# Two semaphores instead of one for the clearing of sixteen row regions

## The reference

```
x = x + 0.5 * moe0(layernorm(x))      # 8 experts, hidden 176, top 2, plus a shared expert of 352
x = x + hgrn(layernorm(x))            # gated linear recurrence, four 256x256 projections
x = x + 0.5 * moe0(layernorm(x))      # the same weights again
x = x + 0.5 * moe1(layernorm(x))      # 16 experts, hidden 128, top 2, plus a shared expert of 128
x = x + attention(layernorm(x))       # 4 heads of 64, sequences of 256
x = x + 0.5 * moe1(layernorm(x))

def moe(X):                           # silu(X W1) * (X W3), then W2, for each chosen expert
    scores = sigmoid(X @ gate); idx = top_k(scores + bias, 2)
    w = scores[idx] / sum(scores[idx])
    return sum_k w[k] * expert[idx[k]](X) + shared(X)
```

## Time and profile before

| what | us |
|---|---|
| runs of the kernel | 882.50, 883.11, 884.25 (median 883.11) |
| profiled execution: span from first to last instruction | 880.5 |
| PE busy in the span | 777.2 (88%) |
| DVE busy | 501.6 (57%) |
| ACT busy | 420.1 (48%) |
| POOL busy | 299.5 (34%) |

### The profile page before, as it was taken

One profiled execution on the slowest core, in us unless ns is written; L12 is line 12 of the kernel. 1 busy time (PEld: TensorE's weight loads), 2 busy tenths in 40 slices (PEclk: granted clock), 3 DMA queues, 4 the chain that ended last, 5 costly groups with the idle time before them and its releaser, 6 DMA issues.

```text
span 880.5 us, 14544 instructions
## 1 busy us (share of the span) xinstructions
PE 777.2 (88%) x3982; PEld 553.5 (63%) x3982; DVE 501.6 (57%) x1737; ACT 420.1 (48%) x1020; POOL 299.5 (34%) x316
## 2 busy tenths in 40 slices
PE   5989999999898996999984699998899886899991
PEld 3446777764465454777752468886677664578881
DVE  4656322368866654322368663227897866663248
ACT  4812334317735711334326436553688777246550
POOL 1570433400000372333314717551011133627560
PEclk9999999999999997999995799999999998899996
DMA  8843333199999523333177235536000011245528
GB/s 297 260 148 104 113 108 96 54 303 366 343 344 341 177 102 119 103 106 104 55 258 299 106 120 178 157 109 222 1 1 2 0 50 42 90 135 185 156 98 290
DMA packets 102364, 135.26 MB, mean 154 GB/s; under 512 B 11366, under 2 KB 90726, under 8 KB 101734
## 3 DMA queue, kind: packets, MB, share of 16 engines
q1 hardware_dynamic: 87894, 95.05, 33.5%
q0 software_dynamic: 14400, 39.34, 12.6%
HBM read 56.23 MB, written 78.12 MB: 153 GB/s over the span
## 4 chain that ended last, share of the span: by engine, by line
PE 64%; DVE 16%; ACT 6%; issue 4%; POOL 4%; DMA 4%; SPq 1%; DVEq 0%; POOLq 0%; ACTq 0%
PE bank L1001 20%; PE bank L1022 12%; PE bank L895 9%; PE bank L981 4%; POOL slot_rows L507 4%; PE bank L1012 3%; PE bank L1067 2%; PE bank L908 2%; DVE X L1295 2%; DVE X L1299 2%; PE bank L835 2%; DVE st L1313 2%; PE bank L1118 2%; DMA Y<-f_result_rows 1%; PE bank L1186 1%
## 5 line engine op out<-in xcount | busy, mean ns | idle before, releaser
L507 POOL DMA_INDIRECT f_result_rows<-arena x172 | 164.8, 958 | 225.6 <-ACT arena L658 124.2
L507 POOL DMA_INDIRECT slot_rows<-XN,slots x128 | 123.8, 967 | 245.9 <-DMA slot_rows<-zeros 120.3
L1001 PE MATMUL bank<-w,arena 128*128 x688 | 204.7, 420 | 0.4 <-ACT arena L645 0.3
L1625 DVE COPY arena<-bank 88x128 f32<-88x128 f32 (+1 forms) x250 | 65.2, 285 | 215.3 <-PE bank L1012 215.2
L1001 PEld LDWEIGHTS bank<-w,arena 128*128 128x128 f32 x688 | 130.4, 191 | 31.7 <-issue 2.4
L1022 PE MATMUL bank<-w,arena 88*128 (+1 forms) x500 | 136.5, 381 | 0.0
L895 PE MATMUL bank<-XT,f_s 128*128 128x512 f32 (+1 forms) x256 | 116.7, 603 | 2.0 <-ACT arena L658 0.9
L652 ACT ACTIVATE arena<-bank 128x128 f32<-128x128 f32 (+1 forms) x172 | 50.8, 295 | 117.3 <-PE bank L1001 117.3
L658 ACT ACTIVATE arena<-bank 128x256 f32<-128x256 f32 x172 | 65.9, 383 | 73.4 <-PE bank L1022 72.6
L1022 PEld LDWEIGHTS bank<-w,arena 88*128 88x128 f32 (+1 forms) x500 | 81.3, 190 | 5.7 <-issue 0.8
L895 PEld LDWEIGHTS bank<-XT,f_s 128*128 128x128 f32 (+1 forms) x256 | 45.7, 186 | 56.3 <-issue 52.8
(11 more groups left out here) (165 smaller groups left out, 1094.8 us busy)
## 6 DMA issues: line engine op xcount, KB each, us to landing
slot_rows<-zeros SPq DMA_DIRECT2D x16, 2176.0 KB, 18.0
arena<-slot_rows SPq DMA_DIRECT2D x172, 128.0 KB, 2.1
XN<-f_result_rows SPq DMA_DIRECT2D x32, 256.0 KB, 5.4
Y<-f_result_rows SPq DMA_DIRECT2D x32, 256.0 KB, 6.1
w<-in_f_w SPq DMA_DIRECT2D x1, 4096.0 KB, 16.3
w<-in_f_w SPq DMA_DIRECT2D x1, 2816.0 KB
f_result_rows<-arena POOLq DMA_INDIRECT x172, 2.5
X<-in_x SPq DMA_DIRECT2D x4, 512.0 KB, 5.4
```

Source lines behind the costliest of these rows:

```text
L507: pool.indirect_dma_start(out=dst, out_offset=bass.IndirectOffsetOnAxis(ap=idx, axis=0), in_=src, in_offset=None).then_inc(done.sem, 16)
L1001: last = pe.matmul(bank[2 + q % 2][:, 0:2 * m.H], xsT[q % 2][:, k, :], L["w13"][:, k, bass.ds(e, 1), :], start=(k == 0), stop=(k == KD - 1))
L1625: last = dve.tensor_copy(hT[q % 2][0:kp, k, :], bank[4 + q % 2][0:kp, k * P:(k + 1) * P])
```

## The change

The one semaphore is replaced by a list of two. Clearing region `e` signals number `e // 8`. POOL's first scatter of stage 2 waits for the first (8 regions), and its first scatter of stage 3 for the second (8 regions). Nothing else differs: on every engine the instructions and their order are the same as before, and of the waits only the two named differ.

```diff
-        regions_zero = sem("regions_zero")
+        regions_zero = [sem("low_regions_zero"), sem("high_regions_zero")]
...
                         sp.dma_start(x_rows[e * SPACE:(e + 1) * SPACE, :].rearrange("(t p) d -> p t d", p=P),
-                                     zeros[:, :].unsqueeze(1).broadcast_to((P, SPACE // P, D))).then_inc(regions_zero, 16)
+                                     zeros[:, :].unsqueeze(1).broadcast_to((P, SPACE // P, D))
+                                     ).then_inc(regions_zero[e // MOE0.E], 16)
...
                     if n == 2 and g == 0:
-                        pool.wait_ge(regions_zero, 16 * MAXE)
+                        pool.wait_ge(regions_zero[0], 16 * MOE0.E)
+                    if n == 3 and g == 0:
+                        pool.wait_ge(regions_zero[1], 16 * (MAXE - MOE0.E))
```

## The result

| kernel | median | lowest to highest | runs |
|---|---|---|---|
| before | 881.58 us | 878.52 to 884.25 | 19 |
| changed | 876.26 us | 872.80 to 881.09 | 19 |

The ratio is 0.9944, 95% interval 0.9929 to 0.9958: the changed kernel is faster by 4.9 us (3.7 to 6.3) where 9.8 had been forecast. Its median lies inside the stated range (870.8 to 876.6), but only because the median of before, 883.11 in the first three runs, is 881.58 in nineteen: applied to 883.11 the ratio gives 878.2. The runs of the changed kernel are also further apart, 8.3 us against 5.7.

What follows compares the result with a forecast made beforehand. Stage 2's late scatters, held by the clearing, were taken to bound the kernel through PE's gap and the slow clock behind it: 8.27 + 1.49 = 9.76 us, median 883.11 to 873.4, range 870.8 to 876.6.

Steps and rivals of the forecast that it cites:

- Low half clear early, new wait free: Stage 2: first eight regions clear by 244.6, 36 us to spare; indices start POOL's scatters at 280.96, the wait costs nothing.
- No cost beside the clearing: Stage 2's eight early scatters keep their pace beside the clearing; cost taken as nothing, beginning only above 2.03 us each.
- rival B: Stage 2: early scatters queue behind the clearing (882 to 883) or POOL stalls while DVE is busy (877.6); chance 0.04.
- Scatter 9 and the last: POOL in stage 2: scatter 9 starts at 297.2 after the third L867, scatter 32 at 326.3 to 327.0 instead of 336.6.
- 8.27 at L981 and 1.49 of slow clock: PE in stage 2: L981 starts 8.27 us earlier, and L981 to L927 takes 12.70 instead of 14.19 us, 1.49 more.
- PE is now the late one: At L981 in stage 2 the first tile is there 1.4 to 2.1 us before PE; some 1.8 of POOL's 10.1 lost.
- High half, stage 3: Clearing ends at most 3.7 us later, at 301.1; stage 3's new wait has 160 us to spare, cost taken as nothing.
- 1 to 2 us of clock scatter: Shifts of slow-clock stretches in later stages, either way, and scatter of runs: 1 to 2 us around the forecast.
- Rival A: Clock dip ahead of stage 2's loop, first 24 L908 taking 7.14 instead of 5.46 us: price 1.7, 875.1; chance 0.10.
- W: Experiments' theory: before's wait for the clearing hides PE's upstream losses in the gap before L981; changed, they reach the end.
- D: Experiments' theory: the missing gain is lost behind the loop of stage 2, as new clock dips.
- Rival C: Slower: shifted work makes PE lose clock in a later stage, at most 7.5 us a stretch; 885 or more, chance 0.02.

Runs made afterwards that it cites:

- high_late: Changed kernel with the clearing of regions 8 to 15 issued behind stage 2's loads: 933.83 us, 1.0580 of the kernel before on its chip.
- after_s3: The changed kernel, unedited, run again on an 882 chip: 875.43 us, 0.9935 of the kernel before there.
- after_warm: Changed kernel with 16 dummy transposes on PE at each of two idle places in stage 1: 875.66 us, 0.9922 of the kernel before there.
- before_warm: Kernel before with 16 dummy transposes on PE at each of two idle places in stage 1: 882.24 us, 1.0004 of the kernel before there.
- after_late: Changed kernel with stage 2's first scatter held back until the third L870, on chip 6: 883.15 us, 1.0019 of the kernel before there.
- after_late_s: Changed kernel with stage 2's first scatter held back until the third L870, on chip 7: 883.57 us, 1.0024 of the kernel before there.
- before_third: The kernel before, unedited, run again on a 911 chip: 909.93 us, 1.0008 of the kernel before there.
- after_third: The changed kernel, unedited, run again on a 911 chip: 901.55 us, 0.9912 of the kernel before there.
- before_pad_third: Kernel before with 64 instead of 24 dummy transposes on PE ending stage 1, on a 911 chip: 914.14 us, 1.0056 of the kernel before there.

## Why the prediction was half right

**Low half clear early, new wait free: right.** Scatter 1 is released by the indices; it started at 282.92 and not 280.96, since stage 2 started 2.0 us late.

**No cost beside the clearing, against rival B: right.** 1.27 us a step against 1.286 forecast, at a DMA share of 1.03 and with DVE busy 6.45 of the 11 us from 282 on. The Trainium skill's round-robin between queues, a packet at a time ("DMA: Bandwidth & Descriptors", "Queues, rings and completion order"), agrees as to this pace of 1.27, and as to the packets from 288 on, where scatters and clearing move side by side (31% and 69% of the DMA engines' time). In the 5 us before, from scatter 1's start at 282.92, none of the scatters' packets moved. Of the Trainium skill's lock-out of GpSimd by DVE ("SBUF — State Buffer", "Who interferes with whom") the same 1.27 shows no sign here either.

**Scatter 9 and the last: right.** 299.20 and 328.28, forecast 297.2 and 326.3 to 327.0, less the 2.0 of the late stage start.

**8.27 at L981 and 1.49 of slow clock: right from stage 2's own start**, 8.1 and 9.6 in sum. The step "PE is now the late one" holds: no gap.

**High half, stage 3: right.** No wait for the clearing is seen there, and high_late shows what it would look like if it came.

**The failed step** is the last: "The span goes from 880.5 to 870.7, the median from 883.11 to 873.4". It takes the difference worked out from one profile for that of the medians. In the profile of before, stage 1 had one dip (PEclk 0.71 at 192 to 196) and neither the one at 240 nor the one in the first L908, and its time doesn't tell whether that was usual, since its gap hides them. Stage 2 started at 270.4, the earliest of the six profiles with an unedited stage 1 (the others 270.9 to 272.6). The forecast put the gapless loop behind this lucky start. The term that was mis-sized is the 1 to 2 us of clock scatter "either way": measured, it is 3 to 4 us between the best runs and the median, and it is nearly all a loss, since the forecast already had full clock in most of these stretches. Three profiles of the changed kernel on 882 chips (two unedited, one warmed) show the loss against the forecast. The first lost 2.0 us ahead of stage 2. after_s3 lost 1.5 there and 1.7 in the first L911. after_warm lost 1.7 in the first L911, after starting stage 2 1.1 us earlier. What the last two lost behind the loop follows below. Rival A named the dip in the first L911 and gave it 0.10; it is there in four of the eight profiles on 882 chips. In before it costs little, since it goes into the gap (8.10 to 5.56 in before_warm).

**The fastest runs reach the forecast time, not the forecast gain.** Five of the six with the clock at 0.960 or 0.961 have spans of 870.2 to 871.5, the sixth 872.2; forecast 870.7. But the fastest of before are faster than its profile as well. Fastest against fastest, the gain is 5.7 us on the first chip (878.52 and 872.80) and 7.2 on chip 7 (879.19 and 872.01).

**What stays open** is how the missing 5 us divide. An estimate from the few profiles there are: stage 2 starts 1.7 us later than in the profile of before on the mean of the other five with an unedited stage 1; the dip in the first L908, 1.7 us in half of the profiles, is 0.85; what is lost behind the loop is 1.6 on the mean of three; and the profile of before stands 0.8 above its median (span 880.5 against 879.7). That is some 4.9 in all, and 9.8 less 4.9 is the 4.9 measured. That it comes out so exactly is luck, with so few profiles. By this estimate W has about half of it and D a third.

Behind the loop, two of three profiles of early scatters on 882 chips lost 2.0 and 2.7 us about the start of the attention stage (526.9 and 527.6 us from the marks' matmuls to the end), none of four with late scatters did (525.0 to 525.1). Rival C had this mechanism, at 0.02 and only as a large loss. Whether these dips come from the earlier phase of the work or by chance, seven profiles don't settle. That W acts is read in before_warm, in the pair of after_late and after_late_s, and in the first profile of the changed kernel; that it is the larger part was not shown.

## What to carry to other kernels

Before a gap is counted as gain, ask what it hides. A wait with a fixed end absorbs every fluctuation ahead of it, and with it removed they can reach the end: expect the median to gain less than one profile promises, and the spread to grow (here from 1.7 to 2.7 us). Take the spread of what stands upstream from more than one profile, and price it as a loss, not as scatter either way.

## What the runs showed of the hardware

Three of the six chips ran the same program 3% slower, 911 for 882 us, with engines standing still for 2 to 9 us at places where they run through on the others. ACT's timeline in before_third, in the first part of stage 2:

```profile
305.20 0.60 ACT L614 ACTIVATE arena<-bank 128x512 f32<-128x512 f32 x1
316.54 0.28 ACT L596 ACTIVATE arena<-bank 128x128 f32<-128x128 f32 x1 [9.21 <-remote]
...
322.24 0.20 ACT L601 ACTIVATE arena<-bank 128x32 f32<-128x32 f32 x1 [4.13 <-remote]
```

In the kernel before on the first chip the same L596 starts at 302.33 without an idle time before it. And in after_third, on the chip of before_third:

```profile
311.22 0.28 ACT L599 ACTIVATE arena<-bank 128x128 f32<-128x128 f32 x1 [4.94 <-remote]
...
312.81 0.20 ACT L604 ACTIVATE arena<-bank 128x32 f32<-128x32 f32 x1
```

The share of the chain that such waits hold, on the page of before_third:

```profile
PE 61%; DVE 15%; ACT 7%; issue 5%; DMA 4%; another core or an unknown queue 4%; POOL 2%; SPq 1%; DVEq 0%; POOLq 0%; ACTq 0%
```

With late scatters these stops are longer: from the start of stage 2 to the second 24 L908 it is 69.2 to 70.6 us in four of the five profiles of before there, padded or not, and 67.4 in the fifth (before_pad_third); in the changed kernel it is 59.5 to 60.4, and on the 882 chips 57.5 to 59.3. That is the 10 us that the change gains on these chips, in front of the loop instead of in the gap. What the engines wait for there, and why it takes longer with late scatters, is open.
